# First attention layer of a fused decoder: probabilities times values as 32-column tiles with 512 columns moving, row sums beside them

## What is computed

```
xn = layernorm(x)                                   # (8, 128, 512)
q = (xn  @ Wq).reshape(b, 128, 32 heads, 16)
k = (ctx @ Wk).reshape(b, 128, 8 kv heads, 16)      # four query heads share one kv head
v = (ctx @ Wv).reshape(b, 128, 8 kv heads, 16)
p = softmax(q . k / sqrt(16), over the 128 context tokens)
a = (p . v).reshape(b, 128, 512)
x = x + tanh(g_xattn[0]) * (a @ Wo)
```

## Time and profile before

| | |
|---|---|
| median of 3 launches | 2903.7 us (2899.5 to 2909.0) |
| profiled execution, its own time | 2922.4 us |
| its span | 2920.6 us |
| TensorE busy | 2796.1 us (96%), 14928 matmul records |
| VectorE busy | 1738.2 us (60%) |
| ScalarE busy | 1044.6 us (36%) |
| GpSimd busy | 826.1 us (28%) |
| mean granted clock of TensorE | 0.978 of full |
| chain of work that ended last | TensorE 90%, VectorE 6%, ScalarE 2% |

### The profile page before, as it was taken

The page is one execution under the profiler, slowest core; times in us unless marked ns, Lnnn a source line. Parts: engine busy times, 40 slices in busy tenths (PEclk is TensorE's granted clock), DMA queues, the critical chain, the costliest instruction groups (busy, mean ns, idle before and its releaser), DMA issues.

```text
span 2920.6 us, 46999 instructions
## 1 busy us (share of the span) xinstructions
PE 2796.1 (96%) x14928; PEld 2352.5 (81%) x14928; DVE 1738.2 (60%) x3969; ACT 1044.6 (36%) x2823; POOL 826.1 (28%) x712
## 2 busy tenths in 40 slices
PE   7997899999999998888999999989999999999998
PEld 5885788888888887667888888878878888888886
DVE  6565645545545546666777777845552555555557
ACT  3441333333333333133444444421123444444442
POOL 5002324333432432323222222235533222212200
PEclk8799999999999999999999999999999999999999
DMA  4001101111111111111000110112111110000000
GB/s 144 12 1 64 36 27 54 36 36 43 40 43 32 47 36 30 37 30 37 30 29 29 29 29 29 30 40 58 58 48 37 30 27 26 26 27 26 28 6 30
DMA packets 59826, 106.35 MB, mean 36 GB/s; under 512 B 7184, under 2 KB 11536, under 8 KB 59536
## 3 DMA queue, kind: packets, MB, share of 16 engines
q1 hardware_dynamic: 56448, 96.49, 11.5%
q10 hardware_dynamic: 3216, 7.81, 0.7%
HBM read 100.09 MB, written 2.10 MB: 35 GB/s over the span
## 4 chain that ended last, share of the span: by engine, by line
PE 90%; DVE 6%; ACT 2%; issue 2%; POOL 0%; DMA 0%; ACTq 0%; DVEq 0%; POOLq 0%
PE four L583 51%; PE outp L583 23%; PE value L583 9%; PE turned L926 4%; PE turned L705 1%; DVE stats L1550 1%; DVE xt_lo L1579 1%; PE turned L630 0%; DVE nt L1522 0%; DVE nt L1524 0%; DVE probs L1574 0%; DVE x L1752 0%; DVE x L1958 0%; ACT sq L1302 0%; ACT vc L1199 0%
## 5 line engine op out<-in xcount | busy, mean ns | idle before, releaser
L556 POOL TENSOR_TENSOR w_hi<-raw,zero 128x512 fp32r<-128x512 f32 x352 | 375.1, 1066 | 1946.6 <-PE four L583 896.3
L1752 DVE SCALAR_TENSOR_TENSOR x<-outp,g_inv,x 128x512 f32<-128x512 f32 x768 | 556.6, 748 | 383.0 <-PE outp L583 382.6
L560 POOL TENSOR_TENSOR w_lo<-raw,w_hi 128x512 fp32r<-128x512 f32 x352 | 453.8, 1289 | 27.6
L583 PE MATMUL four<-xt_hi,w_lo 128*128 128x512 f32 x1024 | 425.2, 415 | 17.0 <-DVE xt_lo L1579 12.0
L583 PE MATMUL four<-xt_hi,w_hi 128*128 128x512 f32 x1024 | 407.0, 397 | 0.0
L583 PE MATMUL four<-xt_lo,w_hi 128*128 128x512 f32 x1024 | 404.4, 395 | 0.0
L583 PE MATMUL outp<-w_hi,a_lo 128*128 128x512 f32 x800 | 329.8, 412 | 14.4 <-DVE x L1752 7.6
L1199 ACT ACTIVATE pT<-turned 128x512 f32<-128x512 f32 x320 | 191.3, 598 | 361.5 <-PE turned L926 286.2
L583 PE MATMUL outp<-w_hi,a_hi 128*128 128x512 f32 x800 | 315.5, 394 | 0.0
L583 PE MATMUL outp<-w_lo,a_hi 128*128 128x512 f32 x800 | 314.8, 393 | 0.0
L1381 ACT ACTIVATE probs<-probs,top 128x128 f32<-128x128 f32 x512 | 199.6, 391 | 237.9 <-DVE top L1795 126.3
(11 more groups left out here) (257 smaller groups left out, 4644.6 us busy)
## 6 DMA issues: line engine op xcount, KB each, us to landing
raw<-in_stream SPq DMA_DIRECT2D x352, 256.0 KB, 2.6
ctx_raw<-in_ctx_t ACTq DMA_DIRECT2D x4, 512.0 KB, 5.8
x<-in_x_in ACTq DMA_DIRECT2D x2, 1024.0 KB, 11.8
kz<-kT SPq DMA_DIRECT2D x32, 64.0 KB, 2.3
pb<-in_position_bias ACTq DMA_DIRECT2D x1, 2048.0 KB, 8.6
out<-x SPq DMA_DIRECT2D x8, 256.0 KB, 2.0
qw<-in_qweight ACTq DMA_DIRECT2D x1, 768.0 KB, 4.0
ln_w<-in_ln_weight ACTq DMA_DIRECT2D x1, 256.0 KB, 2.7
```

Of the source, the lines that this page charges most:

```text
L556: pool.tensor_tensor(w_hi[:, k, :], raw[:, k % RAW, :], zero[:, :].to_broadcast([P, D]), ALU.add)\
L560: pool.tensor_tensor(w_lo[:, k, :], raw[:, k % RAW, :], f32(w_hi[:, k, :]), ALU.subtract)\
L583: m = pe.matmul(out_, l, r, start=start, stop=stop, skip_group_check=True)
L1752: dve.scalar_tensor_tensor(out=x[:, b, :], in0=O[no_f(k) % 2][:, :], scalar=scale, in1=x[:, b, :], op0=ALU.mult, op1=ALU.add)\
```

## The change

- **Values.** For each kv head one matmul replaces four: the stationary operand is now 32 columns (`vv`: the 16 columns of v, at columns 0 to 15 for kv heads 0 to 3 and at 16 to 31 for the others, zeros beside them), and the 512 columns of `pT` move. Four kv heads go to the four groups of 32 partitions of one bank, and the second four are added to the same rows. The result stands feature by row, so no transpose of it is needed: `attended_turn` is gone.
- **Row sums.** The same four matmuls are made with a stationary block of ones (`ones_by_half`) into O[1]. Each sum is there 16 times, once for each row of its head.
- **Division.** VectorE takes the reciprocal of the whole 128x512 bank of sums and multiplies the bank of values with it, once for a batch (`normed(b)`), in place of twice 16 reciprocals and twice 256 products. `a_hi` and `a_lo` are then made from `an` in SBUF, not from PSUM.
- **Wo.** The rows of the result now stand in another order, so the four chunks of Wo are loaded with their rows permuted, by eight DMAs of 16 rows each.
- **Exponentials.** For two of a unit's eight heads ScalarE takes scores and negated maximum straight from PSUM and the `top` tile (two exponentials of 128 columns, called `direct`); VectorE subtracts for the other six (768 columns) and ScalarE's other exponential is over 768.
- `pT` has six buffers, not two. The output of a batch, its addition and its statistics come one to three steps later, and the pipeline has three steps more. `scores(k)` also waits for `direct` of the unit before. At the start there are larger tiles to clear.

```diff
-SPLIT_FIRST = 10
+SPLIT_FIRST = 14
+PARTS = 8
...
-        self.steps = 4 * B + 6
+        self.steps = 4 * B + 9
...
-                "va": sb("va", [P, B, 8, 17], F32, st),
+                "vv": sb("vv", [P, B, 8, 32], F32, st),
+                "ones": sb("ones_by_half", [P, 2, 32], F32, st),
...
+            A0["pT"] = sb("pT0", [P, 6, D], F32, st)
...
-            A0["pT"] = sb("pT0", [P, 2, D], F32, st)
...
+            def load_outputs(j):
+                c = CHUNK_AT[("L0", ("o", j))]
+                first = CHUNK_AT[("L0", ("o", 0))]
+                sp.wait_ge(w_done, c - RAW + 1)
+                for no in range(PARTS):
+                    hh, cg = no // 4, no % 4
+                    row, src = 32 * cg + 16 * hh, 64 * (cg % 2) + 16 * j
+                    sp.dma_start(raw[row:row + 16, c % RAW, :], stream[first + 2 * hh + cg // 2, src:src + 16, :])\
+                        .then_inc(raw_in[c % RAW], 16)
...
                    if u:
                        pe.wait_ge(s["sub"], u)
+                        pe.wait_ge(s["direct"], u)
...
-                def values(g):
-                    b, kv = g // 8, g % 8
-                    side, no = kv // 4, kv % 4
-                    pe.wait_ge(s["pT"], g + 1)
-                    if no == 0 and b:
-                        pe.wait_ge(s["normed"], 2 * (b - 1) + side + 1)
-                    if no == 0 and not b:
+                def values(b, hh, sums):
+                    pe.wait_ge(s["pT"], 8 * b + 4 * hh + 4)
+                    if hh == 0 and b:
+                        pe.wait_ge(s["normed"], b)
+                    if hh == 0 and not b:
                         pe.wait_ge(s["j_out"], 12)
-                    for j in range(4):
-                        o = (4 * no + j) * 17
-                        m = mm((V, O[1])[side][:, o:o + 17], buf["pT"][:, g % 2, tokens(j)],
-                               buf["va"][:, b, kv, :], True, True)
-                        if j < 3:
+                    for cg in range(4):
+                        kv = 4 * hh + cg
+                        w = buf["ones"][:, hh, :] if sums else buf["vv"][:, b, kv, :]
+                        m = mm((V, O[1])[sums][32 * cg:32 * cg + 32, :], w, buf["pT"][:, (8 * b + kv) % 6, :],
+                               hh == 0, hh == 1)
+                        if cg < 3:
                             told(m)
-                    m.then_inc(s["values"], 1)
-                def attended_turn(b):
-                    pe.wait_ge(s["normed"], 2 * b + 2)
-                    if b:
-                        pe.wait_ge(s["x_acc"], b)
-                    for c in range(KT):
-                        m = pe.transpose(O[0][:, tokens(c)], buf["an"][:, tokens(c)], ident[:, :])
-                    m.then_inc(s["a_turned"], 1)
...
-                    g, b = 2 * (k - 2), (k - 7) // 4
-                    if 0 <= g < 2 * L.UNITS:
-                        turn(g)
-                    if 1 <= g <= 2 * L.UNITS:
-                        values(g - 1)
-                    if k >= 7 and k % 4 == 3 and b < B:
-                        attended_turn(b)
-                    if 0 <= g < 2 * L.UNITS:
-                        turn(g + 1)
-                        values(g)
-                    if k >= 8 and k % 4 in (0, 1):
-                        output((k - 8) // 4, k % 4)
+                    u, r = k - 2, k % 4
+                    if 0 <= u < L.UNITS:
+                        turn(2 * u)
+                    if r in (0, 2) and 4 <= k <= L.UNITS + 2:
+                        values((k - 4) // 4, r // 2, 0)
+                    if r in (1, 3) and 9 <= k:
+                        output((k - 9) // 4, r // 2)
+                    if 0 <= u < L.UNITS:
+                        turn(2 * u + 1)
+                    if r in (0, 2) and 4 <= k <= L.UNITS + 2:
+                        values((k - 4) // 4, r // 2, 1)
...
-                    if g >= 2:
-                        act.wait_ge(s["values"], g - 1)
-                    copy(buf["pT"][:, g % 2, :], T[:, :]).then_inc(s["pT"], 1)
+                    if g >= 6:
+                        act.wait_ge(s["values"], (g - 6) // 4 + 1)
+                    copy(buf["pT"][:, g % 6, :], T[:, :]).then_inc(s["pT"], 1)
...
-                    copy(buf["va"][:, 4 * t:4 * t + 4, :, 0:16],
-                         TV[t][:, :].rearrange("p (b h d) -> p b h d", b=4, h=8)).then_inc(s["v_rows"], 1)
+                    rows = TV[t][:, :].rearrange("p (b h d) -> p b h d", b=4, h=8)
+                    copy(buf["vv"][:, 4 * t:4 * t + 4, 0:4, 0:16], rows[:, :, 0:4, :])
+                    copy(buf["vv"][:, 4 * t:4 * t + 4, 4:8, 16:32], rows[:, :, 4:8, :]).then_inc(s["v_rows"], 1)
...
-                    g, b = 2 * (k - 2), (k - 7) // 4
-                    if 0 <= g < 2 * L.UNITS:
-                        turned_out(g)
-                    if k >= 7 and k % 4 == 3 and b < B:
-                        act.wait_ge(s["a_turned"], b + 1)
+                    u = k - 2
+                    if 0 <= u < L.UNITS:
+                        turned_out(2 * u)
+                    if k < L.UNITS:
+                        act.wait_ge(s["top"], k + 1)
+                        for e in range(2):
+                            o = act.activation(buf["pr"][:, k % 3, (6 + e) * P:(7 + e) * P],
+                                               four[:, 3, e * P:(e + 1) * P], ACT.Exp,
+                                               bias=buf["top"][:, k % 2, 6 + e:7 + e], scale=1.0)
+                        o.then_inc(s["direct"], 1)
+                    if k >= 7 and k % 4 == 3 and (k - 7) // 4 < B:
+                        b = (k - 7) // 4
+                        act.wait_ge(s["normed"], b + 1)
                         if b:
                             act.wait_ge(s["outp"], b)
-                        copy(buf["a_hi"][:, :], O[0][:, :]).then_inc(s["a_hi"], 1)
-                    if 0 <= g < 2 * L.UNITS:
-                        turned_out(g + 1)
+                        copy(buf["a_hi"][:, :], buf["an"][:, :]).then_inc(s["a_hi"], 1)
+                    if 0 <= u < L.UNITS:
+                        turned_out(2 * u + 1)
                     if k < L.UNITS:
                         act.wait_ge(s["sub"], k + 1)
-                        p = buf["pr"][:, k % 3, :]
-                        act.activation(p, p, ACT.Exp).then_inc(s["exp"], 1)
+                        cols = buf["pr"][:, k % 3, 0:6 * P]
+                        act.activation(cols, cols, ACT.Exp).then_inc(s["exp"], 1)
...
-                    then(dve.tensor_reduce(top_, src, AX_X, ALU.max))
                     if u >= 3:
                         dve.wait_ge(s["turned"], 2 * (u - 3) + 2)
                     elif u == 0:
-                        dve.wait_ge(ctx_done, KT)
-                    dve.tensor_tensor(buf["pr"][:, u % 3, :].rearrange("p (a e t) -> p a e t", a=4, e=2), src,
-                                      top_.unsqueeze(3).to_broadcast([P, 4, 2, P]), ALU.subtract)\
+                        dve.wait_ge(kz_in[0], 8 * 16)
+                        dve.wait_ge(kz_in[1], 24 * 16)
+                    dve.tensor_reduce(top_, src, AX_X, ALU.max, negate=True).then_inc(s["top"], 1)
+                    dve.wait_ge(s["top"], u + 1)
+                    dve.tensor_tensor(buf["pr"][:, u % 3, 0:6 * P].rearrange("p (a e t) -> p a e t", a=3, e=2),
+                                      src[:, 0:3], top_[:, 0:3].unsqueeze(3).to_broadcast([P, 3, 2, P]), ALU.add)\
                         .then_inc(s["sub"], 1)
-                def normed(b, side):
-                    no = 2 * b + side
-                    dve.wait_ge(s["values"], 4 * no + 4)
-                    v = (V, O[1])[side][:, 0:16 * 17].rearrange("p (h c) -> p h c", c=17)
-                    inv_ = buf["inv"][:, side, :]
-                    then(dve.reciprocal(inv_, v[:, :, 16]))
-                    if b:
-                        dve.wait_ge(s["a_turned"], b)
-                    dve.tensor_tensor(buf["an"][:, side * 2 * P:(side + 1) * 2 * P].rearrange("p (h d) -> p h d", d=16),
-                                      v[:, :, 0:16], inv_.unsqueeze(2).to_broadcast([P, 16, 16]), ALU.mult)\
-                        .then_inc(s["normed"], 1)
+                def normed(b):
+                    dve.wait_ge(s["values"], 2 * b + 2)
+                    then(dve.reciprocal(buf["an"][:, :], O[1][:, :]))
+                    dve.tensor_tensor(buf["an"][:, :], V[:, :], buf["an"][:, :], ALU.mult).then_inc(s["normed"], 1)
                 dve.memset(buf["kz"][:, :, :, :], 0.0).then_inc(s["cleared"], 1)
-                dve.memset(buf["va"][:, :, :, :], 1.0).then_inc(s["cleared"], 1)
+                dve.memset(buf["vv"][:, :, :, :], 0.0).then_inc(s["cleared"], 1)
+                then(dve.memset(buf["ones"][:, :, :], 0.0))
+                for hh in range(2):
+                    then(dve.memset(buf["ones"][:, hh, 16 * hh:16 * hh + 16], 1.0))
...
-                    if k >= 4 and k % 4 in (0, 2) and (k - 4) // 4 < B:
```

(60 more changed lines are left out.)

8 lines of the change are left out of this document (removed).

## The result

The changed kernel takes 2939.4 us (median of 4 launches, 2937.1 to 2940.4) against 2902.9 for the kernel before: a ratio of 1.0105, 95% interval 1.0071 to 1.0139. Timed again beside other launches of before it took 2934.3 us, ratio 1.0097 (1.008 to 1.0113). It is slower by 1%, 28 to 37 us. The forecast was 2916, which is 12 us over the kernel before, with its own range at 2906 to 2936: the direction holds, but the measured difference is between two and three times the forecast one. The first median lies 3 us above that range and 1 us above the outer end of 2938; the second lies inside both.

What follows compares the result with a forecast made beforehand. TensorE bounds the kernel before; afterwards a chain through VectorE's reciprocal, 17.3 us a batch. Terms 1.4 + 3.3 - 6 + 1.5 + 2.2 + 10 = +12.4 us, put on the median: 2916 us; own range 2906 to 2936, outer 2882 to 2938.

Steps and rivals of the forecast that it cites:

- Tiles side by side: TensorE's new groups of values: four column tiles run at once, 1.08 us a group; one after another 3.7.
- Rival 3: TensorE's column tiles don't run side by side: 24.4 us a batch, +59 us (2962); chance 0.12.
- Reciprocal: VectorE's reciprocal over 512 columns, once a batch: 3.0 us, bounds 0.69 and 3.8.
- rival 2: VectorE's reciprocal is short, 0.69 us: chain 15.0 us, -16 us (2888), or -26 (2878) with the clock up early; chance 0.15.
- estimate of 4.2 us by eight passes: VectorE's reciprocal as an iterative divide repeated eight times at 1.0 ns; the forecast sum would end 8 us higher.
- The chain: Reciprocal, product, maximum, subtraction, then TensorE's steps, once round a batch: 17.3 us against 17.05; six rounds, +1.5 us.
- Clock: TensorE's 3 us gap each batch drops its clock, 1.5 us lost, seven times: +10 us, bounds 0 and +20.
- Rival 1: TensorE's clock holds after the gaps: +2.4 us (2906), or -7.6 (2896) if it also comes back early; chance 0.27.
- Steps 3 to 8: Early pipeline stretch before the first output, taken at the lower clock: 34.7 us against 40.7, -6 us.
- The last batch: End of the pipeline, from reciprocal to first output matmul: 5.1 us against 2.9, +2.2 us.
- ScalarE's two waits: At the first steps scores wait for `direct` behind ScalarE's copy of q, twice: +3.3 us.
- the start: Clearing larger tiles delays TensorE's first low part of the context; with two more short ScalarE copies, +1.4 us.

Runs made afterwards that it cites:

- filled gap: Changed kernel with three zero-adding 128x512 matmuls put ahead of the scores of units 8, 12, .. 28: 2916.9 us, ratio to before 1.0028.
- second profile of before: The kernel before, profiled once more with no edit: 2902.9 us, last addition of attention 1 at 209.64 us.
- first profile of before: The kernel before, unedited, in the profile the forecast was made from: 2922.4 us, with a half-clock stretch of 40.7 us.
- halved version: Changed kernel with each batch's reciprocal cut into two of 256 columns behind successive subtractions, high and low parts a step later: 2916.2 us, ratio to before 1.0028.

## Why the prediction was right in direction and short in size

- **Tiles side by side:** right, 1.06 us against 1.08 forecast and 3.7 estimated for one after another, and TensorE busy for 13.87 us a batch against 13.9 forecast. Rival 3 is out.
- **Reciprocal:** 3.36 us against 3.0. The slope of 4.5 ns a column above a product's was low; 3358 - 691 = 2667 ns over 512 columns is 5.2. The bounds (0.69 and 3.8) held, rival 2 is out. The estimate of 4.2 us by eight passes, from the Trainium skill, "VectorE: DVE Perf Modes", section "First, the fixed hardware budget", is high by 0.8.
- **The chain:** right in its order, 17.36 to 17.47 us a round at full clock against 17.3; the gap is 3.47 us instead of 3 for the reciprocal's 0.36.
- **Clock:** the drops come right behind the gaps, as forecast. Chain and clock together were put at +11.5 us for attention 1; five batches alone measured +11.4 in one profile and +15.0 in the other (100.2 against 85.2). The filled gap shows the clock's share to be 13 to 17 us in all, inside the 0 to 20, where +10 was taken. Rival 1 is out: the clock fell behind five of the six gaps in one profile and behind all six in the other.
- **Steps 3 to 8: the step that failed.** "I take it as low until the first output again", -6 us, and then "I put the same difference on the median". The reason given, "The clock falls there for light work", does not hold: the second profile of before ran the same 203 records at 1.00, and the changed kernel ran its lighter units 3 to 6 at 1.00 too (74.79 to 88.90 us). Nor was it only light work ahead of that stretch: scores, transposes and 17-column matmuls stood alone for 3.6 us (67.85 to 71.49), and the 12 us before them were almost wholly 512-column matmuls of q. What brought the fall in that execution stays open. The right pair was full against full, 24.5 us by the text's own figure against 22.4, so +2 and not -6. It measured 26.4 because the clock fell behind the gap ahead of unit 8: that unit took 5.7 us (granted clock 0.63) where the filled version took 3.9, which belongs to the clock's term. The profile's 19 us over the median was the sign: an execution that is 19 us long has something in it that the median lacks, and that something was the 40.7 us row. This one term is 8 of the missing 20 us.
- **The last batch: mis-sized.** +2.2 was meant for the way from the reciprocal to the first output matmul, which took 2.9 and takes 6.3 (234.19 - 227.91): 0.4 more for the reciprocal, and VectorE's addition of the batch before (233.30), which the matmul waits for and which stands behind `a_lo`. Not counted at all: behind the gap of 4.75 us ahead of them the twelve output matmuls run at the lower level (0.63 us each where 0.39 is usual), 5.5 us instead of 3.1; and the gap and fall ahead of it, at 212 us, another 3.4. Together +9.3, so 7 us short.
- **ScalarE's two waits** (+3.3) and the start (+1.4): +2.4 and +1 to +3.3.

With +2 for -6 and +9.3 for +2.2 the sum is +27.5, against 30 measured in attention 1; that it comes so near is partly luck, since the clock's share measured 3 to 7 us more than the +10, and some of it already stands in the last batch's +9.3. The failed step made the forecast smaller, so the direction does not rest on it.

## What to carry over

Before a difference found on a profile is put on a median, ask what the profiled execution has that the median lacks; a stretch at half clock that equals the excess is no base for a term. Count, too, how many of the timed launches are as long. A long instruction costs by its place in the queue: find which maximum, scores or other step waits behind it, and where in the cycle the engine is free. The same 3.4 us a batch are a loss of 30 us in the chain and none once they are cut up and stand where VectorE is free, and once the chain is out of the way, TensorE's savings count. Count the end of a pipeline by itself, with its own order and its own clock.

## What was not expected of the hardware

- The same gap does not always cost the clock. In the first profile of the changed kernel a gap of 3.47 us ahead of 114.92 was followed by 1.00, the ones ahead of 132.39 and 151.44 by a fall; in its second profile all from unit 8 on brought one. The long fall of the first profile of before (0.50 for 40.7 us) had no gap of TensorE in it, and in the 3.6 us ahead of it only one of 0.81 us, which stands in the second profile of before as well. In the halved version a gap of 1.27 to 1.29 us brought a fall in every other batch. Without the reciprocal one gap of 1.22 us was followed by a step of 6.8 us, while all later ones, 0.80 to 0.82, brought nothing, nor did the 0.69 to 0.71 of the filled version. What decides between equal gaps stays open.
- Three matmuls that add zero, 2.74 us of TensorE in a gap of 3.47, made the kernel faster by 17 us or more.
- Equal code after attention 1 took 2681 to 2696 us in eleven profiles. A single profile of this kernel cannot tell a change of 10 us from none, unless it is read by its parts.
